# The scores for the row maximum as two half-height matmuls side by side in the first layer

## The reference

```python
qkv = jnp.einsum('oc,bchw->bohw', w_qkv, x)
q, k, v = jnp.split(qkv, 3, axis=1)             # to heads: [b, 8, 1024, 48]
att = jnp.einsum('bhxd,bhyd->bhxy', q * scale, k)
att = jax.nn.softmax(att, axis=-1)
out = jnp.einsum('bhxy,bhyd->bhxd', att, v)
out = jnp.einsum('oc,bchw->bohw', w_proj, out) + b_proj[None, :, None, None]
```

## Time and profile before

| what | value |
| --- | --- |
| time, median of 3 runs | 6341.27 us (6335.64 to 6345.97) |
| the profiled execution | 6352.18 us, of which the span from first to last instruction is 6350.4 us |
| granted TensorE clock, mean over the span | 0.951 of full speed |
| busy over the span | PE 90%, PEld 63%, DVE 76%, ACT 61%, POOL 10% |
| layer 0, stretch 100 to 1830 us | PE 1618.49 us, DVE 1492.86 us, ACT 1237.50 us busy |

### The profile page before, as it was taken

The page is one execution under the profiler, slowest core; times in us unless marked ns, Lnnn a source line. Parts: engine busy times, 40 slices in busy tenths (PEclk is TensorE's granted clock), DMA queues, the critical chain, the costliest instruction groups (busy, mean ns, idle before and its releaser), DMA issues. The chain is left out here.

```text
span 6350.4 us, 121429 instructions
## 1 busy us (share of the span) xinstructions
PE 5693.4 (90%) x45900; PEld 3982.8 (63%) x45900; DVE 4855.1 (76%) x10150; ACT 3901.0 (61%) x5362; POOL 663.3 (10%) x802
## 2 busy tenths in 40 slices
PE   5999999999968988999989989899998997899798
PEld 2455554555434557885568865688755786555688
DVE  5888888888865789887799977898878988343333
ACT  3777766777652557885578855688755886121242
POOL 2111211111102001011010010110001100000000
PEclk9999999999988999999999999999999998999898
DMA  4212221222114544555455554555454554111698
GB/s 146 66 55 56 64 59 43 65 67 60 39 54 113 123 117 112 129 119 123 108 124 122 123 129 109 120 123 122 109 135 110 125 123 118 66 60 40 156 235 200
DMA packets 197671, 661.96 MB, mean 104 GB/s; under 512 B 62985, under 2 KB 64833, under 8 KB 154243
## 3 DMA queue, kind: packets, MB, share of 16 engines
q1 hardware_dynamic: 172723, 603.24, 38.6%
q0 software_dynamic: 24320, 50.37, 3.2%
HBM read 540.04 MB, written 62.71 MB: 95 GB/s over the span
## 5 line engine op out<-in xcount | busy, mean ns | idle before, releaser
L2428 PE MATMUL b_near_p<-b_near_work,b_near_hkt 64*128 64x144 f32 (+37 forms) x27520 | 2118.5, 309 | 257.1 <-DVE b_near_acc L2302 161.6
L2428 PEld LDWEIGHTS b_near_p<-b_near_work,b_near_hkt 64*128 64x128 f32 x27520 | 1969.5, 195 | 469.0 <-DVE b_near_work L2373 286.9
L2373 DVE TENSOR_TENSOR b_near_work<-b_near_work 128x140 f32<-128x140 f32 (+26 forms) x5312 | 1610.7, 354 | 218.8 <-PE b_near_p L2428 133.7
L2273 ACT ACTIVATE b_near_work<-b_near_work,b_near_mcol 128x512 f32<-128x512 f32 (+6 forms) x1328 | 765.1, 647 | 860.5 <-DVE b_near_work L2373 779.6
L2277 ACT ACTIVATE b_near_work<-b_near_work,b_near_mrow 128x544 f32<-128x544 f32 (+6 forms) x1328 | 762.5, 646 | 0.0
L539 ACT ACTIVATE a_ex<-a_p_t 128x1024 f32<-128x1024 f32 x512 | 524.2, 1024 | 365.2 <-PE a_p_t L477 364.1
L614 DVE TENSOR_REDUCE a_nm<-a_p_x 128x1 f16<-128x1024 f32 x512 | 625.6, 1222 | 154.5 <-PE a_p_x L466 147.7
L2302 DVE SCALAR_TENSOR_TENSOR b_near_acc<-b_near_p,b_near_dwc,b_near_acc 128x323 f32<-128x323 f32 (+14 forms) x1088 | 622.1, 574 | 157.4 <-PE b_near_p L2428 155.8
L1812 PE MATMUL b_near_p<-b_near_hp,b_near_ow 128*98 128x480 f32 (+14 forms) x1568 | 658.2, 570 | 0.0
L620 DVE TENSOR_TENSOR a_el<-a_ex,a_eh 128x1024 f16<-128x1024 f32 x512 | 621.7, 1214 | 8.0 <-ACT a_eh L544 6.9
L544 ACT CAST a_eh<-a_ex 128x1024 f16<-128x1024 f32 x512 | 535.4, 1046 | 50.8
(11 more groups left out here) (225 smaller groups left out, 5635.2 us busy)
## 6 DMA issues: line engine op xcount, KB each, us to landing
b_near_work<-sampling_positions_near SPq DMA_DIRECT2D x666, 512.0 KB, 6.5
d_win<-merged_kernels SPq DMA_DIRECT2D x192, 263.0 KB, 6.7
b_near_xin<-x SPq DMA_DIRECT2D x24, 1024.0 KB, 8.2
a_xr<-in_x SPq DMA_DIRECT2D x12, 1536.0 KB, 6.4
a_xh<-in_x SPq DMA_DIRECT2D x9, 1536.0 KB, 6.5
x<-a_xr SPq DMA_DIRECT2D x9, 1536.0 KB, 5.7
b_near_xr<-x SPq DMA_DIRECT2D x13, 1024.0 KB, 15.9
x<-b_near_xr SPq DMA_DIRECT2D x13, 1024.0 KB, 4.7
```

Source lines behind the costliest of these rows:

```text
L2273: last = e.activation(rx[:, u, xo[c]:xo[c + 1]].rearrange("p (a b) -> p a b", a=H), pp[:, b, 1, :].rearrange("p (a b) -> p a b", a=H)[:, : ...
L2373: e.tensor_tensor(S[:, k % NS, 0:(r1 - r0) * w].rearrange("p (a b) -> p a b", b=w), rx[:, u, xo[cc]:xo[cc + 1]].rearrange("p (a b) -> p a ...
L2428: last = e.matmul(G[:, a0 - top:z0 - top, c0 - left:c1 - left], hkt[64 * s:64 * s + 64, SIDE * cr + cc, :], S[64 * s:64 * s + 64, k % NS, ...
```

## The change

The maximum is computed from the high halves alone, over 48 rows instead of 96. The first half of the keys is multiplied on rows 0 to 47 with `q`, the second half on rows 64 to 111 with a copy of q's high half in a new tile `qx`. To that end all tiles get the layout of 112 rows: high half on 0 to 47, low half on 64 to 111, the row of maxima and the row of ones at 48, zeros (ones in `kh`) up to 63. `turned` now multiplies 112 rows in each of its four matmuls. The copy `qx` adds one DMA to each piece. `oh` is laid out on the rows of `ROWS_OF`, `o` is dropped: the product with `denb` is written over `osum`, and the wait for the pack DMA of the head two earlier moves from L641 to the addition L605, four slots earlier. POOL fills 32 rows of `kh`, `q` and `kl` at the start, where it filled one row of `kh`.

```diff
-    MAXROW = 2 * D
+    MAXROW = D
+    ROWS = 64 + D
...
-    MOVES = [16 * 6 * len(pieces) for pieces in PIECES]
+    MOVES = [16 * 7 * len(pieces) for pieces in PIECES]
...
-                e.memset(kh[MAXROW:MAXROW + 1, :, :], 1.0).then_inc(s_fill.sem, 1)
-                e.wait_ge(s_fill.sem, s_fill.at(2))
                 e.memset(v[:, :, :, SUMROW:SUMROW + 1], 1.0).then_inc(s_fill.sem, 1)
-                e.wait_ge(s_fill.sem, s_fill.at(3))
+                for n, (rows, value) in enumerate(((kh, 1.0), (q, 0.0), (kl, 0.0))):
+                    e.wait_ge(s_fill.sem, s_fill.at(2 + n))
+                    e.memset(rows[32:64, :, :], value).then_inc(s_fill.sem, 1)
+                e.wait_ge(s_fill.sem, s_fill.at(5))
...
                     if s == QUERY:
-                        e.dma_start(q[part * D + d0:part * D + d1, hd, :], rows).then_inc(s_block[j].sem, 16)
+                        e.dma_start(q[64 * part + d0:64 * part + d1, hd, :], rows).then_inc(s_block[j].sem, 16)
+                        if part == 0:
+                            e.dma_start(qx[64 + d0:64 + d1, hd, :], rows).then_inc(s_block[j].sem, 16)
                     else:
-                        for z in (0, D):
+                        for z in (0, 64):
...
-                    for n in range(2):
-                        last = e.matmul(p_x[:, n, :], q[0:MAXROW, hd, :].rearrange("r (p c) -> r p c", c=NT)[:, :, c],
-                                        kh[0:MAXROW, hd, n * HALF:(n + 1) * HALF], start=True, stop=True)
+                    for n, (r, high) in enumerate(((0, q), (64, qx))):
+                        last = e.matmul(p_x[:, n, :], high[r:r + D, hd, :].rearrange("r (p c) -> r p c", c=NT)[:, :, c],
+                                        kh[r:r + D, hd, n * HALF:(n + 1) * HALF], start=True, stop=True)
...
-                        for kk, r in ((kh, MAXROW + 1), (kl, MAXROW)):
-                            last = e.matmul(p_t[:, n, :], kk[0:r, hd, c * P:(c + 1) * P],
-                                            q[0:r, hd, n * HALF:(n + 1) * HALF], start=(r > MAXROW), stop=(r == MAXROW))
+                        for r, kk in enumerate((kh, kl)):
+                            last = e.matmul(p_t[:, n, :], kk[:, hd, c * P:(c + 1) * P],
+                                            q[:, hd, n * HALF:(n + 1) * HALF], start=(r == 0), stop=(r == 1))
...
+                        if hh >= 2 or not isinstance(b, int) or b > 0:
+                            e.wait_ge(s_packed[p].sem, s_packed[p].at(...))
                         for i, n in enumerate(order(k)):
                             e.wait_ge(s_oa.sem, s_oa.at(b * (2 * HEADS) + 2 * hh + 1 + i))
-                            e.tensor_tensor(osum[r:r + D, n, :], (p_o[1] if n else p_o[2 * (hh % 2)])[64:TP, :], oh[0:D, hh % 2, n, :], ALU.add).then_inc(s_on.sem, 1)
+                            e.tensor_tensor(osum[r:r + D, n, :], (p_o[1] if n else p_o[2 * (hh % 2)])[64:TP, :], oh[r:r + D, n, :], ALU.add).then_inc(s_on.sem, 1)
...
-                        if hh >= 2 or not isinstance(b, int) or b > 0:
-                            e.wait_ge(s_packed[p].sem, s_packed[p].at(...))
                         e.sem_inc(sh["tick"], 1)
-                        e.tensor_tensor(o[r:r + D, :], osum[r:r + D, :, :].rearrange("p n q -> p (n q)"), denb[r:r + D, :], ALU.mult).then_inc(s_n.sem, 1)
+                        e.tensor_tensor(osum[r:r + D, :, :].rearrange("p n q -> p (n q)"), osum[r:r + D, :, :].rearrange("p n q -> p (n q)"), denb[r:r + D, :], ALU.mult).then_inc(s_n.sem, 1)
```

More of the change, by code:

```diff
@@ L228, in layer0 @@
         split = a.sb("split", [P, 2, 2, N], F16)
-        q = a.sb("q", [MAXROW + 1, HEADS, N], F16)
-        kh = a.sb("kh", [MAXROW + 1, HEADS, N], F16)
-        kl = a.sb("kl", [MAXROW, HEADS, N], F16)
+        q = a.sb("q", [ROWS, HEADS, N], F16)
+        qx = a.sb("qx", [ROWS, HEADS, N], F16)
+        kh = a.sb("kh", [ROWS, HEADS, N], F16)
+        kl = a.sb("kl", [ROWS, HEADS, N], F16)
         v = a.sb("v", [P, NT, HEADS, TP], F16)
@@ L236, in layer0 @@
         el = a.sb("el", [P, WR, N], F16)
-        oh = a.sb("oh", [64, 2, 2, HALF])
+        oh = a.sb("oh", [P, 2, HALF])
         osum = a.sb("osum", [TP, 2, HALF])
@@ L240, in layer0 @@
         denb = a.sb("denb", [TP, N])
-        o = a.sb("o", [TP, N])
         packed = a.sb("packed", [P, G3, N])
@@ L418, in image @@
                         e.sem_inc(sh["tick"], 1)
-                        e.dma_start(den[:, hh % 2, :], oh[SUMROW:SUMROW + 1, hh % 2, :, :].rearrange("o n q -> o (n q)")).then_inc(s_d2.sem, 16)
+                        e.dma_start(den[:, hh % 2, :], oh[ROWS_OF[hh % 2] + SUMROW:ROWS_OF[hh % 2] + SUMROW + 1, :, :].rearrange("o n q -> o (n q)")).then_inc(s_d2.sem, 16)
                         e.wait_ge(s_rc.sem, s_rc.at(b * HEADS + hh + 1))
@@ L551, in slot @@
                             e.wait_ge(s_d2.sem, s_d2.at(at(b, HEADS * 16, (hh - 1) * 16)))
-                            e.copy(oh[:, hh % 2, n, :], (p_o[1] if n else p_o[2 * (hh % 2)])[0:64, :]).then_inc(s_oa.sem, 1)
+                            e.copy(oh[ROWS_OF[hh % 2]:ROWS_OF[hh % 2] + 64, n, :], (p_o[1] if n else p_o[2 * (hh % 2)])[0:64, :]).then_inc(s_oa.sem, 1)
                     for ahead, unit in done_at(m - 1, end):
@@ L577, in slot @@
                         for j, d0, d1, r in PACK[hh % HEADS]:
-                            e.dma_start(packed[r:r + d1 - d0, j, :], o[ROWS_OF[hh % 2] + d0:ROWS_OF[hh % 2] + d1, :]).then_inc(s_packed[hh % 2].sem, 16)
+                            e.dma_start(packed[r:r + d1 - d0, j, :], osum[ROWS_OF[hh % 2] + d0:ROWS_OF[hh % 2] + d1, :, :].rearrange("p n q -> p (n q)")).then_inc(s_packed[hh % 2].sem, 16)
                 for m in range(BEGIN, FIRST):
@@ L601, in slot @@
                         hh = k // NT
-                        r = ROWS_OF[hh % 2]
+                        r, p = ROWS_OF[hh % 2], hh % 2
+                        if hh >= 2 or not isinstance(b, int) or b > 0:
+                            e.wait_ge(s_packed[p].sem, s_packed[p].at(b * PACKED[p] + hh // HEADS * PACKED[p] + 16 * sum(len(PACK[hd]) for hd in range(p, hh % HEADS, 2))))
                         for i, n in enumerate(order(k)):
                             e.wait_ge(s_oa.sem, s_oa.at(b * (2 * HEADS) + 2 * hh + 1 + i))
-                            e.tensor_tensor(osum[r:r + D, n, :], (p_o[1] if n else p_o[2 * (hh % 2)])[64:TP, :], oh[0:D, hh % 2, n, :], ALU.add).then_inc(s_on.sem, 1)
+                            e.tensor_tensor(osum[r:r + D, n, :], (p_o[1] if n else p_o[2 * (hh % 2)])[64:TP, :], oh[r:r + D, n, :], ALU.add).then_inc(s_on.sem, 1)
                     for i, part in outs_at(m - 1) if m > FIRST else ():
@@ L635, in slot @@
                         hh = k // NT
-                        r, p = ROWS_OF[hh % 2], hh % 2
+                        r = ROWS_OF[hh % 2]
                         e.wait_ge(s_d4.sem, s_d4.at((b * HEADS + hh + 1) * 16))
-                        if hh >= 2 or not isinstance(b, int) or b > 0:
-                            e.wait_ge(s_packed[p].sem, s_packed[p].at(b * PACKED[p] + hh // HEADS * PACKED[p] + 16 * sum(len(PACK[hd]) for hd in range(p, hh % HEADS, 2))))
                         e.sem_inc(sh["tick"], 1)
-                        e.tensor_tensor(o[r:r + D, :], osum[r:r + D, :, :].rearrange("p n q -> p (n q)"), denb[r:r + D, :], ALU.mult).then_inc(s_n.sem, 1)
+                        e.tensor_tensor(osum[r:r + D, :, :].rearrange("p n q -> p (n q)"), osum[r:r + D, :, :].rearrange("p n q -> p (n q)"), denb[r:r + D, :], ALU.mult).then_inc(s_n.sem, 1)
                 def statistics(b):
```

## The result

The changed kernel takes 6372.6 us (median of 5 runs, 6371.34 to 6375.01), against 6341.27: 1.0049 times the time before, with a 95% interval of 1.0035 to 1.0064, or 31 us more. The forecast was 6375 us. The profiled execution after took 6372.3 us with a span of 6370.5 us; its granted clock is 0.951, as before. The two profiles are only 20.1 us apart, because the profiled execution before was 10.9 us slower than its median.

The account below looks back on a forecast made before the run. PE was taken to bound 379 layer 0 slots, with DVE near full; the half-row pair adds 0.09 us in each, +34 us on the 6341.3 us median, giving 6375 us, with 6334 to 6412 for 8 in 10.

Parts of the forecast that it names:

- The pair overlaps: Layer 0 scores: the two 48-row matmuls run at the same time, 0.22 us instead of 0.44.
- The borders: Changing between full and half rows around the score pair drains TensorE: 0.10 us in and 0.10 out.
- the first rival: Faster: borders cost only what float16 loads leave, the pair takes 0.22 instead of 0.44 us; 62 us gained, 6279; chance 0.12.
- The exposed weight loads: At the pair's borders, matmuls wait for float16 weights: 0.07 us going in, 0.04 coming back, scaled down from float32.
- The slots that count: 379 layer 0 slots with a projection, set by PE, pay the pair's 0.09 us; the other 133 absorb it.
- The reduction starts as before: DVE's reduction of the scores: the pair starts 0.17 us late but ends sooner, so its start and DVE's work stay.
- The moved wait: Head addition waiting for the pack two heads earlier: no cost, cover 0.4 to 1.1 us at the image boundaries.
- the prediction's own last sentence: Signs of being wrong: loads start ahead, the pair doesn't overlap, or the image-boundary addition starts behind a DMA.
- The 7th DMA: One more DMA per piece, 80 issues of 0.50 us on POOL: no cost, ACT's wait for `split` unchanged.
- The price of the stall as such: ACT's wait in layer 0 for the DMAs out of `split` costs PE 4.6 us.
- The fills: POOL's start: one fill of 6.92 us becomes three, ending at about 33.6 us, under DVE's statistics ending at 43.96.
- Edits that cost nothing: Added DMA, start fills, `oh`/`osum` layout, in-place product and moved wait: held to add nothing to the time.

Follow-up runs that it names:

- out_only: Kernel before with only the output edits (`oh` on its head's rows, product written over `osum`, pack wait moved to the addition): 6363.3 us, ratio 1.0027.
- split_wait: Kernel before, full-height scores, with separate semaphores for the DMAs of q and k, so each waits only for its own: 6293.1 us, ratio 0.9916.
- full_rows: Changed kernel with full-height score matmuls, `qx` zero on rows 0 to 63, and one more fill at the start: 6364.0 us, 1.0024 times the kernel before.
- after_pad26: Changed kernel with 26 semaphore increments that nothing waits for on DVE at the start: 6354.4 us, 1.0016 times the kernel before.
- pad6: Kernel before with six semaphore increments that nothing waits for on DVE at the start: 6357.5 us, ratio 1.0017.
- pad32: Kernel before with 32 semaphore increments that nothing waits for on DVE at the start: 6339.4 us, ratio 0.9992.

## Why the forecast came out right, and where its steps did not

The forecast said 34 us more and it was 31, but the closeness is luck: the one term it had was too large by some 20 us, and terms of about the same size that it had at nothing were missing.

- **The pair overlaps** (taken as such): right. 3 ns between the starts; without the overlap the time is 77 us longer by the ratios, 82 by the medians.
- **The borders**, 0.10 us each way: right, 98 ns going in, and 367 - 213 - 54 = 100 ns coming back. The Trainium skill, "TensorEngine Tiling (Array Packing)", Key Properties, states that a change of mode drains TensorE; this trace agrees and gives the price. The speedup of up to 2x that the same page of the Trainium skill gives under Theoretical Speedup was the first rival; the two streams do overlap wholly, but among full-height matmuls nothing is gained. That rival is out.
- **The exposed weight loads**, 0.07 and 0.04 us: too large. They are 54 ns (a score matmul lasts 433 instead of 379) and 10 ns (389 instead of 379 for the first `turned`). With 0.054 and 0.010 in the same sum, and 0.213 for the stream where the forecast had 0.22, the pair costs 0.475 us against 0.435: this is the mis-sized term, 0.09 us where the trace has 0.04. Scaling down the float32 loads a bit more than with their duration wasn't enough; the float16 load of the scores exposed half of what the float32 one did (54 of 104 ns), and the one behind it an eighth (10 of 80).
- **The slots that count**, 379: right in number, 382 are longer. But those at a head's end were among them (3.80 and 3.81 us after, 3.78 before), which the forecast held to stay, and the plain slot grew by 32 ns to 3.06 or 3.07 us, not to 3.12. 382 x 0.032 = 12 us, for a term of 34.
- **"The reduction starts as before"**: it starts 0.63 us behind the start of the scores instead of 0.79, which is 0.07 us earlier in the slot. Two slots near heads' ends in most images are 0.09 us shorter, 1.6 us in all, which fits it.
- **The moved wait**, at nothing with a cover of 0.4 to 1.1 us: right to 2.4 us, but the cover did go. After the change, DVE waits for the DMA at four of seven image boundaries:

```profile
863.45 0.69 DVE L611 TENSOR_TENSOR a_osum<-a_p_o,a_oh 48x512 f32<-48x512 f32 x1 [1.09 <-DMA a_packed<-a_osum]
```

  The pack here landed 4.6 us after its start at 858.36, where the rows before showed 3.4. All idle time in front of this line at the seven boundaries is 4.8 us after and 2.4 us before, so the wait cost 2.4 us at most. By the prediction's own last sentence this was a sign of being wrong, and the argument behind it, that both times follow from one event and can't move against each other, doesn't hold. In out_only, where the wait is moved too, no addition starts behind the DMA.
- **The 7th DMA**, at nothing since the k DMAs' "number and start stay" and no queue was seen to reach them: this step failed. Six times in the eight images, POOL stands still for 1.61 us in the middle of the k DMAs that ACT waits for, with no semaphore behind it. Then the starts of the 16 issues span 8.95 us instead of 7.33. All four kernels with `qx` have it; of those without it, five pause there in one image alone (2.04 us before), and split_wait pauses six times for 1.13 us among other k DMAs, which nothing waits for. So a pause isn't peculiar to 7 DMAs, but with them it fell where it costs. Why POOL pauses stays open. After:

```profile
754.61 0.50 POOL L377 DMA_DIRECT2D a_kl<-a_split  x1 [1.61 <-issue]
```

  The waits of ACT for `split` (us in total, times, longest), after and then before:

```profile
ACT a_split L348 <- DMA a_kl<-a_split: 46.1, 8, 8.3
```

```profile
ACT a_split L346 <- DMA a_kl<-a_split: 41.2, 8, 8.3
```

  PE's idle time in front of `turned` at this place is 28.3 us in seven images after and 23.2 before, 5 us more; full_rows and after_pad26 have it too, out_only doesn't. The price of the stall as such was right only for one image (4.6 us); in the other six it was 2.9 to 3.5.
- **The fills**: hidden, as said; the first scores start at 88.9 us after and at 89.6 before.
- **"Edits that cost nothing"** had no term for the code itself. Six more instructions on DVE, which came with the moved wait, shifted the code of layer 1's loop, and DVE idled at its top. Only the profiles and the padding runs showed it: 13.7 us more in the loop of layer 1 after the change, and 13 and 17 us of the time in the runs of pad6 and out_only. Nor had it one for L148, 2.9 us.

What the idle time at the top of a loop is, is argued, not shown. The Trainium skill, "Runtime: NRT & Kernel Launch", Instruction fetch mechanics, states that instructions stream in by blocks and that a taken branch to a block that isn't held makes the engine wait for its fetch. The runs agree in that the idle comes right behind a loop's branch, has no semaphore behind it, and moves when code is shifted. But the place of DVE's code alone doesn't decide: split_wait executes as many DVE instructions as the kernel before (14727 in the trace), and only PE and ACT have more (72 and 21, none of them busy), and it shows no idle time where the kernel before had 3.6 and 3.2 us. What else decides stays open. It wasn't tried to shift one of the other engines alone.

## What to carry to other kernels

A half-height pair saves one stream and pays for two borders and two late weight loads; among full-height float16 matmuls of 512 columns that is 213 ns against 251, a loss. By the same sum (an estimate) two pairs between the borders would gain, which wasn't tried. When the change in a measured time is the size of one stall at a loop's top, compare the parts of the program that weren't touched first, and run the old kernel with dummy instructions before believing in any mechanism. That nobody waits for an added DMA doesn't make it free: look at what the same engine issues behind it. The largest gain lay in neither: a wait that counted DMAs it didn't need.

## What the runs showed of the hardware that wasn't expected

- Six semaphore increments at the start of a program lengthened it by 0.17% (0.06 to 0.27%), 32 did not lengthen it, and both act on a loop 2 to 5 ms later. With idle times of 3.2 to 7.0 us at one to three of the three returns to the loop's top, a difference of 13 to 18 us can come from this alone (pad6 against the kernel before and against pad32).
- A float16 weight load behind a change to half rows delayed its matmul by 54 ns, the one behind the change back by 10 ns, although their own durations are 138 and 100 ns.
- Four `turned` matmuls that all have 112 rows are spaced 215 to 216 ns apart (full_rows), those that go back and forth between 97 and 96 rows 218 to 219. The plain slot of full_rows is 10 ns shorter than before.
- A DVE instruction over 256 numbers lasted 1.8 or 6.6 us beside POOL's fills, and ended within 0.03 us of the end of a fill both times.
